# A vision tower's feed-forward weights loaded by 12 transfers over all chunks in place of 48 by chunk

## What is computed

```python
h = tok(x, conv_w, ...)                       # convolution, layer norm, dense
h = layernorm(h + attention(h))               # 8 heads, two softmaxes, group norm, output projection
# feed-forward, with weights merged for each image from 8 task vectors:
gh = relu(einsum('bsd,hd->bsh', x, gfc1_w) + gfc1_b)
g  = (einsum('bsh,eh->bse', gh, gfc2_w) + gfc2_b).mean(axis=1)
W1m = W1 + einsum('be,efd->bfd', g, tv_W1)    # F = 512, D = 128, E = 8
W2m = W2 + einsum('be,edf->bdf', g, tv_W2)
h1 = relu(einsum('bsd,bfd->bsf', x, W1m) + b1m)
out = einsum('bsf,bdf->bsd', h1, W2m) + b2m
h = layernorm(h + layernorm_affine(x + out))
```

## Time and profile before

| | us |
|---|---|
| median of 3 runs | 248.41 |
| lowest and highest | 246.67, 249.39 |
| profiled execution | 247.2 |
| its span | 245.4 |
| TensorE, VectorE busy | 188.9, 150.7 |

### The profile page before, as it was taken

One profiled execution on the slowest core, in us unless ns is written; L12 is line 12 of the kernel. 1 busy time (PEld: TensorE's weight loads), 2 busy tenths in 40 slices (PEclk: granted clock), 3 DMA queues, 4 the chain that ended last, 5 costly groups with the idle time before them and its releaser, 6 DMA issues.

```text
span 245.4 us, 8170 instructions
## 1 busy us (share of the span) xinstructions
PE 188.9 (77%) x3611; PEld 148.4 (60%) x3611; DVE 150.7 (61%) x335; ACT 105.3 (43%) x185; POOL 47.8 (19%) x64
## 2 busy tenths in 40 slices
PE   0899989967755566888697999999999999993000
PEld 0899965535634455754286777778878887783000
DVE  2342494552989998889764455555555344458970
ACT  2000046560451324123543356777775234335792
POOL 0000008000667685000000000000007000005670
PEclk9999999997999955579965599999999999999555
DMA  7999973234555000000002002020200000000012
GB/s 233 395 391 388 351 126 93 75 87 107 126 125 131 18 3 4 5 0 4 0 3 72 27 24 76 25 79 27 76 3 3 3 3 3 5 3 1 12 57 67
DMA packets 11107, 19.82 MB, mean 81 GB/s; under 512 B 2030, under 2 KB 6830, under 8 KB 10432
## 3 DMA queue, kind: packets, MB, share of 16 engines
q1 hardware_dynamic: 11072, 19.30, 26.7%
HBM read 15.20 MB, written 0.82 MB: 65 GB/s over the span
## 4 chain that ended last, share of the span: by engine, by line
PE 54%; DVE 27%; DMA 4%; issue 4%; ACT 4%; SPq 3%; POOL 2%; ACTq 0%; POOLq 0%
PE PS L1074 16%; PE PS L895 9%; PE PS L1096 9%; DVE arena L302 5%; PE PS L1086 4%; PE PS L932 4%; DVE t L646 4%; PE PS L1123 3%; SPq L363 3%; DMA hid<-arena 2%; ACT t L607 2%; DVE sm L700 2%; DVE st L848 2%; DVE mx L688 2%; PE PS L954 2%
## 5 line engine op out<-in xcount | busy, mean ns | idle before, releaser
L302 DVE COPY arena<-PS 128x1024 f32<-128x1024 f32 x32 | 39.2, 1226 | 46.3 <-PE PS L1074 46.3
L301 ACT ACTIVATE arena<-PS 128x1024 f32<-128x1024 f32 x32 | 34.5, 1078 | 32.7 <-PE PS L1074 32.7
L1074 PE MATMUL PS<-gates,wrow 18*128 18x128 f32 x1024 | 41.1, 304 | 3.0 <-DVE arena L302 1.8
L1074 PEld LDWEIGHTS PS<-gates,wrow 18*128 18x128 f32 x1024 | 35.1, 206 | 10.2 <-DVE arena L302 5.0
L895 PE MATMUL PS<-hid,arena 128*128 128x128 f32 (+1 forms) x208 | 27.4, 293 | 7.3 <-DVE hid L625 7.3
L895 PEld LDWEIGHTS PS<-hid,arena 128*128 128x128 f32 (+1 forms) x208 | 25.9, 202 | 8.7 <-issue 8.3
L1096 PE MATMUL PS<-arena,t 128*32 128x128 f32 x512 | 22.9, 326 | 0.0
L954 PE MATMUL PS<-hid,arena 128*32 128x200 f32 x256 | 13.7, 362 | 10.8 <-DMA hid<-arena 10.7
L1123 PE MATMUL PS<-arena,hid 128*32 128x128 f32 x512 | 21.1, 312 | 0.1
L456 ACT ACTIVATE sd<-mv,epsc 128x2 f32<-128x2 f32 (+1 forms) x15 | 4.3, 293 | 36.4 <-DVE mv L636 36.4
L625 DVE TENSOR_REDUCE hid<-hid 128x256 f32<-128x1280 f32 x4 | 9.5, 2363 | 16.7 <-DMA hid<-conv_filter 16.7
(11 more groups left out here) (104 smaller groups left out, 283.8 us busy)
## 6 DMA issues: line engine op xcount, KB each, us to landing
arena<-windows SPq DMA_DIRECT2D x24, 256.0 KB, 7.7
wrow<-ffn_weights SPq DMA_DIRECT2D x32, 128.0 KB
hid<-arena SPq DMA_DIRECT2D x32, 100.0 KB, 2.2
hid<-conv_filter SPq DMA_DIRECT2D x4, 640.0 KB, 7.1
cst<-consts SPq DMA_DIRECT2D x1, 1098.0 KB, 16.2
wrow<-ffn_weights SPq DMA_DIRECT2D x64, 8.0 KB
out<-t SPq DMA_DIRECT2D x16, 50.0 KB
arena<-windows SPq DMA_DIRECT2D x4, 64.0 KB, 7.9
```

The source lines that it names most:

```text
L301: return eng.activation(dst, PS[:, b:b + 2, :], ACT.Copy)
L302: return eng.tensor_copy(dst, PS[:, b:b + 2, :])
L1074: mm = pe.matmul(PS[:, merge_bank(n) + r, k * P:(k + 1) * P], wrow[32 * r:32 * r + KR, w], gates[32 * r:32 * r + KR, :], start=True, stop= ...
```

## The change

Layer 0's rows are loaded by a new function, `load_first_rows`, on one semaphore. It issues four transfers to 16 partitions each (all four chunks, 64 pieces of 8 KB, 512 KB), one for each r, and then eight to two partitions each (32 pieces of 1 KB, 32 KB), one for each r and each half h of the base rows. The bytes and their places in `wrow` are the same. `load_rows` is renamed `load_chunk` and is used for layer 1 alone. `merge` waits once, at chunk 0, for all 12 transfers; chunks 1 to 3 wait for nothing, and chunks 4 to 7 for the first filling of `wrow_loaded`. The place in SyncE's list is the old one: behind the constants, ahead of the key spreads.

```diff
+        first_rows_loaded = sem("first_rows_loaded")
...
-            def load_rows(m, c):
+            def load_first_rows(m):
+
+                rows = wrow[:, :].rearrange("p (c n) -> p c n", c=NC)
+                for r in range(NR):
+                    tv = tvw_d[2 * m + r % 2].rearrange("(x c z) n -> x c z n", c=NC, z=2)[:, :, r // 2, 0:HE]
+                    sp.dma_start(rows[32 * r:32 * r + RE], tv).then_inc(first_rows_loaded, 16)
+                for r in range(NR):
+                    for h in range(2):
+                        base = tvw_d[2 * m:2 * m + 2, :, HE:HS].rearrange("h (j c r y) n -> j c r y h n", j=NJ, c=NC, r=NR)
+                        dst = wrow[32 * r + RE:32 * r + KR].rearrange("p (c y h n) -> p c y h n", c=NC, y=NR, h=2)
+                        sp.dma_start(dst[:, :, :, h], base[:, :, r, :, h]).then_inc(first_rows_loaded, 16)
+
+            def load_chunk(m, c):
...
-            for c in range(NC):
-                load_rows(0, c)
+            load_first_rows(0)
             for u in range(NU8):
                 spread_keys(u)
             for c in range(NC):
                 sp.wait_ge(merge_done, NQ * (c + 1))
-                load_rows(1, c)
+                load_chunk(1, c)
...
-                if q == 0:
-                    pe.wait_ge(wrow_loaded[cc % NC], 16 * NR * (1 + NJ) * (cc // NC + 1))
+                if cc == 0 and q == 0:
+                    pe.wait_ge(first_rows_loaded, 16 * NR * (1 + NJ))
+                elif cc >= NC and q == 0:
+                    pe.wait_ge(wrow_loaded[cc % NC], 16 * NR * (1 + NJ))
```

## The result

The changed kernel takes 254.41 us in the median (253.11 to 255.20, 4 runs), the kernel before 248.22 beside it (246.67 to 249.39). The ratio is 1.025, with an interval of 1.017 to 1.033: slower, by some 6 us, where 248.7 was forecast and 252.1 was the upper end. The profiled execution is 253.11 us with a span of 251.3, so 5.9 us above that of before in both.

The account below looks back on a forecast made before the run. Late key spreads in SyncE's queue, then VectorE behind the fourth score group, were taken as the bound. +0.45 (scores(0)) + 0.5 (clock) - 0.66 (gap) = +0.3 gave 247.5 us profiled, 248.7 median; range 242.7 to 252.1.

Parts of the forecast that it names:

- The issue of the first spread: SyncE's queue: with its time freed, key spread 0 is issued at 46.24 us rather than 52.38.
- a backlog inside the DMA engines: DMA engines ahead of the key spreads: large pieces drain, then small ones on two engines; spread 0 lands at 57.2 us.
- rival (a): Small transfers don't hold the key spreads: scores(0) starts at 53.05, -5.5 us in all, 242.9 us median; chance 0.20.
- what the clock costs: TensorE after its idle stretch: a later return of the full clock over scores(1) and the value projection, 0.5 us.
- these two engines are free at 55.0: The two DMA engines carrying the small transfers finish at 46 + 9.0 = 55.0 us (52.3 to 62.1).
- I take 46: DMA engines: 2.10 MB of large pieces at 130 GB/s from about 29.5 us are through by 46 us.
- the spreads' 0.070 us a piece: Small pieces on two DMA engines: the key spreads' rate of 0.070 us for 1 KB gives 9.0 us.
- The rest of spread 0: Spread 0's own share on each DMA engine, 1.7 us, and some 0.5 us to the semaphore: landing at 57.2.
- the 0.66 us taken off for VectorE's gap: VectorE before a later score reduction: a 0.66 us wait absorbs that much of the delay to scores(0).
- (c): The two DMA engines bind longer: free at 58.5, +3.7 us, 252.1 us median, +7.4 at the backlog's full rate; chance 0.20.
- The page's port rule: SBUF ports at 27.2 GB/s each: large pieces end at 48.8 us, small ones 9.6 us later at 58.4; about 252 us.

## Why the prediction was wrong

**Right.** The issue of the first spread: 46.24 forecast, 46.06 measured. That the freed queue time would be eaten by a backlog inside the DMA engines, large pieces first, then small pieces on two of sixteen engines: 0.12 and 30 GB/s forecast, 0.14 and 26 measured, and runs with none, half and all of the small pieces confirm it. What the freed time is worth without it: -5.5 forecast for rival (a), where the small transfers behind the spreads show -4.6 and the old 48 there -5.3. And what the clock costs: 0.5 forecast, and from the start of scores(0) to that of the value projection it is 4.70 us after (61.86 to 66.56), 4.18 before (56.80 to 60.98). It didn't reach the end by that way, though, as said below.

**The term that was too small** is "these two engines are free at 55.0". It was two sums, and both were short; the second was the one that mattered.

*The large pieces:* "I take 46". The first 1 KB piece behind them starts at 46.88, so on the two engines in question this was short by 0.9 us. (Of the other engines one has large pieces left until 49.5.) The 130 GB/s came from two windows of 1 us at the backlog's start; the changed kernel has 132 and 91 GB/s in the same two, and 106 to 111 in most of those that follow. The Trainium skill's "SBUF — State Buffer", section Door 1, gives 4 ports of 27.2 GB/s for 16 partitions, 109 GB/s, and the trace agrees from 34 us on. In the kernel before the four partition groups took turns at 128 KB each; whether that made its rows faster was not tried.

*The small pieces:* 9.0 us, from the spreads' 0.070 us a piece. Measured are 13.0 us, from 46.88 to 59.85. Where they run alone the changed kernel has 0.086 us, which for 128 pieces would be 11.0. From 50 to 54 us, beside the spreads on the other engines, a piece takes 0.15 us by its record, and that makes up most of the rest. The run with four engines shows that the number of engines is not the limit. The same page gives one port of 27.2 GB/s for four neighbouring partitions, which agrees with the 26 where the pieces run alone.

So the two engines are free at 59.85 and not at 55.0, 0.9 us by the large pieces and 4.0 by the small. The rest of spread 0, 2.2 us in the forecast, took 1.9, and it landed at 61.73 against 57.2.

**The term that was wrong in kind** is the 0.66 us taken off for VectorE's gap. I took the fourth group's scores as moving less than the first's, "since spread 3 is issued behind spread 2 in either kernel". But spread 2 waits for scores(0), and eight issues and a landing follow in a fixed row up to scores(3). From the end of scores(0) to the landing of spread 3 it is 8.87 us before and 9.29 after. Whatever delays scores(0) delays scores(3) as much: 5.06 and 5.47 us, and VectorE's waits there were 0.55 and 0.46 us after, 0.66 before. This row also passes by scores(1), the value projection and scores(2), where the forecast had put its 0.5 for the clock. So + 5.06 reached the end whole, with some 0.4 us on the row to scores(3) and 0.4 behind VectorE's fourth group, whose cause stays open.

**The rivals.** (c) was the case, with a mechanism as told, and had a chance of 0.20. Its price of +3.7 lay midway between two rows, with +7.4 at the far one; measured +5.9. The range ended at (c)'s midpoint rather than at its far bound, and so missed by 2.3 us. The page's port rule, worked out in the prediction beside (c), gave 58.4 for the moment the two engines are free, against 59.85, and (c) itself 58.5. The rule came that near by two errors that offset: the large pieces through at 48.8 rather than 46.9, the small ones 9.6 us rather than 13.0. And it came to about 252 us in the prediction, inside the range that missed.

## What to carry to other kernels

Merging transfers saves the issuing engine's time, and can cost more inside the DMA engines: ask of each new form how many engines share it and how many partitions it writes to, and what is queued behind its slowest share. A small transfer that the critical path waits for shouldn't stand behind a burst of bulk data that isn't needed for another 70 us. Move the bulk behind it, and leave it slow: here a burst, as far as these traces tell, also held up the loading of instructions, which the profile lists under no wait at all. When a bound is taken from a row, check that the row's mix is that of the new form.

## What was not expected of the hardware

**Bulk transfers delay instruction loading.** With the large pieces issued at 74 to 75 us, TensorE stood still for 9.93 and 10.58 us in two kernels, with matmuls that waited for nothing, and the instruction queue showed no packet for over 10 us while the weights' queue kept all 16 engines busy at 112 GB/s. In the place of the change the same burst delays a fetch too: the kernel before has a 16 KB instruction packet at 37.03 us, and the changed kernel has its next after 21.05 only at 46.72, as the large pieces end. It cost nothing there: TensorE projects on without a gap from 41.78 to 52.75. It starts 77 matmuls from 30 to 47 us in the changed kernel, and 330 from 74 to 88 with all 12 behind the spreads; that it needs few new instructions in the first place is my reading of this, not shown.

That the fetch is held up by the backlog fits all four kernels with bulk behind the spreads, the one with a slow issue included; how the engines choose between the queues was not tried. The Trainium skill's "DMA: Bandwidth & Descriptors", section on queues, rings and completion order, says that an engine takes turns between the queues that it has work for, a whole packet of several descriptors at a time. Whether gaps of 14 and 18 us between instruction packets are such turns, with pieces of 8 KB that take over 1 us each, no run here shows.

**SyncE's issue can stall on a backlog.** Its queue in the changed kernel, 27.9 to 37.6 us:

```profile
27.55 11.95 SPq L351 DMA_DIRECT2D wrow<-ffn_weights  x3
```

Eight small issues took 18.91 us rather than the 5.3 that I forecast, since several waited, one for over 9 us. With the small ones behind the spreads and the large ones long through, the same eight took 5.35. They ended at 44.39, 1.7 us ahead of the spreads' turn, so this cost nothing here; the cause of the stall was not tried further.
